# Convolution kernels made between expert tiles, idle matmuls, and experts joined with their combine in one block

## What is computed

```python
x = x + tanh(g_xattn[i]) * attention_i(layernorm(x), ctx)
x = x + tanh(g_ffn[i]) * ffn_i(layernorm(x))
...
eh = gelu(ln(ctx @ hist_W + hist_b))
aw = softmax(gelu(eh @ ctx_W1 + ctx_b1) @ ctx_W2 + ctx_b2)
cc = sum(eh * aw)
kp = gelu(ln(cc @ kg_W1 + kg_b1)) @ kg_W2 + kg_b2
kernels = softmax(kp.reshape(B, H, 9))
```

## Time and profile before

| what | value |
|---|---|
| median of 3 runs | 862.2 us |
| the profiled execution | 863.15 us |
| its span, first to last instruction | 861.4 us |
| mean granted TensorE clock, share of 2.4 GHz | 0.851 |
| busy: PE, PEld, DVE, ACT, POOL | 73%, 55%, 49%, 34%, 27% |

### The profile page before, as it was taken

How to read it: one execution, slowest core, us unless ns; L and a number is a source line. 1 busy time by engine, 2 the same in 40 slices (tenths; PEclk the granted TensorE clock), 3 DMA queues, 4 the chain that set the end, 5 groups by cost and what they waited for, 6 DMA issues and landing times. The chain is left out here.

```text
span 861.4 us, 14476 instructions
## 1 busy us (share of the span) xinstructions
PE 625.5 (73%) x4568; PEld 474.8 (55%) x4569; DVE 419.9 (49%) x1096; ACT 289.5 (34%) x826; POOL 230.0 (27%) x275
## 2 busy tenths in 40 slices
PE   4888679775199999927963799833977999528771
PEld 2556566455189999913652366511544666414441
DVE  3674456783633333265956233247644453352333
ACT  1285223772044444303420233320631444202220
POOL 2033010132145553110000466303400111115651
PEclk9999899898589999967965899955886999757996
DMA  7970000000110010018500111010000000001122
GB/s 230 356 290 1 1 0 1 2 1 7 38 30 26 25 24 18 13 56 320 172 0 25 34 41 41 27 49 2 1 0 2 2 2 2 5 27 40 43 40 85
DMA packets 28984, 44.77 MB, mean 52 GB/s; under 512 B 5458, under 2 KB 18402, under 8 KB 28674
## 3 DMA queue, kind: packets, MB, share of 16 engines
q1 hardware_dynamic: 24514, 35.02, 12.2%
q0 software_dynamic: 4416, 9.05, 4.1%
HBM read 37.44 MB, written 6.62 MB: 51 GB/s over the span
## 5 line engine op out<-in xcount | busy, mean ns | idle before, releaser
L1105 PE MATMUL experts_ps<-experts_act,experts_own 128*128 128x128 f32 x736 | 86.0, 275 | 0.2 <-ACT experts_act L1160 0.2
L1285 PE MATMUL gated_ps_in<-experts_w_in,gated_slots_t 128*128 x138 | 75.5, 659 | 13.4 <-issue 5.7
L1105 PEld LDWEIGHTS experts_ps<-experts_act,experts_own 128*128 128x128 f32 x736 | 84.0, 192 | 0.3 <-issue 0.3
L1160 ACT ACTIVATE experts_act<-experts_ps,experts_b 128x128 f32<-128x128 f32 x184 | 52.6, 369 | 72.1 <-PE experts_ps L1105 57.4
L1038 POOL DMA_INDIRECT gated_slots<-ffn_tokens,keep_ffn_token x46 | 44.6, 969 | 72.8 <-issue 46.6
L1196 DVE COPY experts_own<-experts_w 128x2048 f32 x23 | 28.2, 1226 | 64.5 <-PE experts_ps L1105 64.5
L642 POOL TENSOR_TENSOR core_e<-core_e,core_inverse 128x1024 f32<-128x1024 f32 x16 | 30.4, 1902 | 103.6 <-DVE core_inverse L787 103.6
L1029 POOL DMA_INDIRECT ffn_results<-gated_results,keep_ffn_row x46 | 45.4, 986 | 37.6 <-DVE gated_results L1381 28.7
L1038 POOL DMA_INDIRECT experts_slots<-ffn_tokens,keep_ffn_token x23 | 36.8, 1599 | 63.1 <-PE experts_ps L1086 41.2
L1371 DVE COPY gated_slots_t<-gated_ps_x 128x128 f32<-128x128 f32 x46 | 13.4, 292 | 82.5 <-PE gated_ps_x L1277 72.3
L1304 PEld LDWEIGHTS gated_ps_y<-experts_w_out,gated_gated_t 128*128 128x128 f32 x276 | 35.9, 197 | 24.4 <-issue 24.4
(11 more groups left out here) (390 smaller groups left out, 1372.6 us busy)
## 6 DMA issues: line engine op xcount, KB each, us to landing
experts_w<-in_L_ffn_W SPq DMA_DIRECT2D x1, 8192.0 KB, 40.2
experts_w_in<-in_gated_in SPq DMA_DIRECT2D x1, 4096.0 KB, 12.3
combine_mine<-ffn_results SPq DMA_DIRECT2D x12, 256.0 KB, 3.5
experts_w<-in_L_ffn_W SPq DMA_DIRECT2D x1, 2048.0 KB, 11.6
experts_w_out<-in_gated_out SPq DMA_DIRECT2D x1, 2048.0 KB, 17.2
ffn_tokens<-route_xn SPq DMA_DIRECT2D x3, 512.0 KB, 3.2
experts_w_in<-in_L_ffn_gate_w SPq DMA_DIRECT2D x1, 1024.0 KB, 7.6
experts_w_in<-in_L_ffn_up_w SPq DMA_DIRECT2D x1, 1024.0 KB, 10.4
```

The lines of the kernel that those rows point to most:

```text
L1105: mm = pe.matmul(ps_2[u][:, c * P:(c + 1) * P], own2[:, u, k, c * P:(c + 1) * P], act1[:, u, k, :], start=(k == 0), stop=(k == chunks - 1))
L1160: act.activation(to[:, u, c, :], source[u][:, c * P:(c + 1) * P], ACT.Gelu, bias=bias[:, bass.ds(e * chunks + c, 1)]).then_inc(done, 1)
L1285: mm = pe.matmul(ps_in[:, banks * u + n], slots_t[:, u, :], w_in[:, bass.ds(e, 1), 512 * n:512 * n + 512].rearrange("d a h -> d (a h)"), s ...
```

## The change

1. `conv_kernels` becomes a class `ConvKernels` whose pieces are called between expert tiles of layer 1's `gelu_experts`. PE has ten pieces, at steps j = 1, 4, 5, 6, 9, 10, 11, 14, 15 and 18, each behind `layer3(j - 2)`; ACT has five (2, 4, 6, 12, 15), DVE thirteen, POOL three (behind the gathers 0, 8 and 18). For this, the loops of PE, ACT and DVE there are written out. It has two PSUM banks instead of eight. The weights for it (13 DMAs, `ConvWeights.load`) are issued by SP in layer 1's `route`, behind the store of the tokens, no longer in the attention of layer 2.
2. `gated_experts` and the combine behind it share one block (`Together`), in layers 2 and 3.
3. `idle_matmuls(pe, keep, bank, times)`: matmuls of 128 x 128 fp32 whose result nobody reads: 16, 10 and 30 in each of three `route`s, 14 at the start of each of three expert stages, 16 in `lora_ffn`, 40 at the end of `latent_operands`.
4. The normalisation in `wide_attention` (attentions 0 and 1) takes `scalar_tensor_tensor` with rstd spread over the row as a second tensor.

```diff
+def idle_matmuls(pe, keep, bank, times):
+    for _ in range(times):
+        pe.matmul(bank[:, 0:P], keep.identity[:], keep.iota[:], start=True, stop=True)
...
-                    dve.tensor_scalar(xn[:, t % ring, :], keep.x[:, t, :], moments[:, t, 0:1], rstd[:, t:t + 1],
-                                      ALU.subtract, ALU.mult).then_inc(sem["xn_ready"], 1)
+                    dve.scalar_tensor_tensor(out=xn[:, t % ring, :], in0=keep.x[:, t, :], scalar=moments[:, t, 0:1],
+                                             in1=rstd[:, t:t + 1].to_broadcast([P, D]), op0=ALU.subtract, op1=ALU.mult)\
+                        .then_inc(sem["xn_ready"], 1)
...
                     .then_inc(sem["tokens_stored"], 16)
+                if load_ahead:
+                    load_ahead(sp)
                 sp.wait_ge(sem["tokens_stored"], 16)
...
             def _(pe):
+                idle_matmuls(pe, keep, ps[:, 2], 16)
                 norm.tensor(pe)
...
                 mm.then_inc(sem["logits_made"], 1)
+                idle_matmuls(pe, keep, ps[:, 2], 10)
                 pe.wait_ge(sem["chosen_ready"], 1)
...
                     .then_inc(sem["counted"], 1)
+                idle_matmuls(pe, keep, ps[:, 2], 30)
                 pe.wait_ge(sem["order_ready"], 1)
...
+                idle_matmuls(pe, keep, ps_y, 14)
                 turn_slots(0, 0, 0, True)
                 layer1(0, 0, True)
                 turn_slots(1, 1, 0)
                 turn_slots(2, 2, 0)
...
-                with pe.Fori(1, (TILES - 3) // 4) as i:
-                    for v in range(2):
-                        steady(i, v)
+                for j in range(1, TILES - 2):
+                    layer1(j, j % 2, j == 1)
+                    layer2(j - 1, (j - 1) % 2, j <= 2)
+                    turn_slots(j + 2, (j + 2) % AHEAD, (j + 2) // AHEAD)
+                    if j >= 2:
+                        layer3(j - 2, j % 2, j == 2)
+                    kernels.tensor(pe, j)
...
+                for j in range(1, TILES - 1):
+                    gelu1(j + 1, (j + 1) % 2)
+                    gelu2(j, j % 2, j == 1)
+                    kernels.scalar(act, j)
...
+                for j in range(1, TILES - 2):
+                    own_weights(j + 1, (j + 1) % 2)
+                    keep_slots(j + 2, j % 2)
+                    if j >= 2:
+                        keep_result(j - 2, (j - 2) % AHEAD, (j - 2) // AHEAD)
+                    kernels.vector(dve, j)
...
+class ConvKernels:
...
+    def tensor(self, pe, j):
...
+        if j == 9:
+            pe.wait_ge(sem["aw_ready"], 1)
+            for u in range(2):
+                mm = pe.matmul(ps[:, 0, u:u + 1], self.aw[:, 2 * u:2 * u + 2, :].rearrange("p b k -> p (b k)"), self.one[:],
+                               start=True, stop=True)
+            mm.then_inc(sem["cols_made"], 1)
...
+    def scalar(self, act, j):
...
+        if j == 6:
+            act.wait_ge(sem["aw_centred"], 1)
+            act.activation(self.aw[:], self.aw[:], ACT.Exp).then_inc(sem["aw_exp"], 1)
...
                 mm.then_inc(sem["v_made"], 1)
+                idle_matmuls(pe, keep, ps[:, 2], 40)
...
-                    gated_experts(nc, keep, "gated2", keep.routes[1], w_in2, w_out2, loaded2, 32)
-                with Together(nc), Scope(nc, "combine2") as c:
-                    conv_kernels(nc, keep, "kernels3", conv_weights, taps, Combine(keep, c, keep.routes[1]), rows3)
+                with Together(nc) as block, Scope(nc, "combine2") as c:
+                    combine = Combine(keep, c, keep.routes[1])
                     gated_experts(nc, keep, "gated2", keep.routes[1], w_in2, w_out2, loaded2, 32)
+                    block.sync(combine.load)
+                    combine.add(block, rows3)
...
-            gated_experts(nc, keep, "gated3", keep.routes[2], w_in3, w_out3, loaded3, 48)
-        with Together(nc) as block, Scope(nc, "combine3") as c:
-            combine = Combine(keep, c, keep.routes[2], out)
-            combine.add(block)
+            with Together(nc) as block, Scope(nc, "combine3") as c:
+                combine = Combine(keep, c, keep.routes[2], out)
+                gated_experts(nc, keep, "gated3", keep.routes[2], w_in3, w_out3, loaded3, 48)
+                combine.add(block)
```

468 lines of the change are left out of this document (221 added, 247 removed).

## The result

| what | before | after |
|---|---|---|
| median | 862.1 us (4 runs, 858.91 to 863.43) | 840.45 us (4 runs, 839.9 to 842.73) |
| profiled execution's span | 861.4 us | 840.9 us |
| mean granted TensorE clock | 0.851 | 0.919 |
| busy: PE, PEld, DVE, ACT, POOL | 73, 55, 49, 34, 27% | 81, 63, 50, 35, 27% |

The ratio is 0.9754, with a 95% interval of 0.9731 to 0.9777: 21 us less. The forecast was 827, 35 us less; the time lies 1.6 us inside the slow end of its range (842).

A forecast was written before the change was run, and what follows sets the result against it. No single bound: PE in layer 1's experts, chains of small steps at seams and routes, and PE's low clock behind waits. Terms -21.0 + 6.0 - 2.0 - 16.5 - 1.5 = -35.0 from 863.15 give 828.1, 827 against the median; range 814 to 842.

The forecast's parts named there:

- part 4: Layer 3's combine in the experts' block: its load goes out at 848.7 instead of 850.8, -2.0 us (0 to -3).
- Part 1: Between layer 2's experts and layer 3's attention: the convolution kernels' block goes, the combine stays, gain 21.0 us (19 to 22).
- keeps its 2.85 us: After layer 2's combine, the way into layer 3's attention, a branch on the mask, takes 2.85 us as before.
- Part 2: Convolution kernels' work moved into layer 1's experts, where PE is the limit: +6.0 us, bounds 5 and 13.2.
- So nothing waits: Layer 1's experts: DVE and ACT have 3 us free per tile, so the pieces cause no waits.
- Part 3: Layer 1's experts: writing the loops out changes nothing, 0 us; results come 5.47 us apart either way.
- Part 5: Idle matmuls in routes, `lora_ffn`, layer 2's attention and expert starts raise PE's clock: -16.5 us (0 to -20).
- The clock need not fall: Layer 1's route: 16, 10 and 30 idle matmuls take 3.9, 2.4 and 7.2 us and fit their gaps.
- rival (b): Idle matmuls do no harm but give little, since DVE or a DMA sets each start: 840 us, chance 0.14.
- Part 6: Wide attentions: normalisation with two tensors takes 0.35 us where three took up to 1.97, -1.5 us (0 to -5).
- Rival (d): Loops: waits in layer 3's experts may hang on code position, and go (818) or reach another loop (838); chance 0.14.

The follow-up runs named there:

- the load ahead: Changed kernel with layer 2's combine loads issued in the experts' block and its adds in a block of their own: 840.4 us, ratio 0.975.
- the jump taken out: Changed kernel, joined block kept, without the attention for any mask that is jumped over when the mask is causal: 837.6 us, ratio 0.979.

## Why the prediction came out as it did

The direction and the main cause were right; the size was not: 21 us instead of 35. The time is inside the range, but near its end: the two largest terms and two of the others all erred to the slow side, and only part 4 gave more than forecast. By its own steps:

- **Part 1 (-21.0): -18.0 measured**, 39.25 to 21.24 us from the last result to the attention. Load, landing and combine came as worked out, the load even 0.7 us sooner. The step that failed is "keeps its 2.85 us": it is 6.43, and 6.41 to 6.43 in all eight profiles with the joined block and the jump. The forecast took the end of the combine's block as it was. But the joined block ends with the long DRAIN on POOL, 3.84 us behind POOL's last work, where the combine's own block has 0.06. The join did not remove this time, it moved it from ahead of the load to ahead of the attention. That the indirect DMAs call for it is the likeliest reading, since only the blocks with them have it; no run leaves them out, and what POOL does in that time no record shows.
- **Part 2 (+6.0): +7.9 measured** from first to last result, and 0.9 ahead of it: +8.8, inside its bounds. Records of PE in the pieces:

```profile
243.00:372.00 129.00, 7.32 (x41) 4.70 (x41) 4.02 (x11) 0.47 (x1) 1.00 0.08 21
```

  They are 7.32 us (the piece of j = 1 included) where half of 13.22 is 6.6, and the latency at the end of a piece, which the forecast gave to other matmuls to cover, isn't given back: the step with the piece of j = 9, four small records of 0.60 us in all, is 0.73 us longer than 5.47. "So nothing waits" failed once, at j = 2: the normalisation on DVE waits for POOL, and the next weights come behind it.

```profile
257.15 0.73 DVE L1647 TENSOR_SCALAR experts_eh<-experts_eh,experts_eh_moments,experts_eh_rstd 128x256 f32<-128x256 f32 x2 [2.56 <-POOL experts_eh_rstd L1535]
...
260.04 1.13 PE L1109 MATMUL experts_ps<-experts_slots_t,experts_own 128*128 128x128 f32 x8 [0.75 <-issue]
```

  That cost 1.0 us over two steps. The place where a wait was most likely, the Exp with its two table loads at j = 6, held as worked out (ACT's timeline):

```profile
284.82 1.28 ACT L1615 ACT_TABLE_LOAD   x1
286.11 0.42 ACT L1615 ACTIVATE experts_aw<-experts_aw 1x256 f32<-1x256 f32 x1
286.55 1.28 ACT L1167 ACT_TABLE_LOAD   x1
287.84 2.43 ACT L1167 ACTIVATE experts_act<-experts_ps,experts_b 128x128 f32<-128x128 f32 x8
```

  1.28 + 0.42 + 1.28 = 3.0 us, and the two results behind it come 5.47 us apart as in the loop. The Trainium skill gives 2.66 us per switch, of which 1.38 are a drain ("ScalarE: Activation LUTs", What ACT_TABLE_LOAD costs). This trace has the 1.28 us of the load and no drain: each instruction in these lines starts 0.01 to 0.02 us behind the one before.
- **Part 3 (0): 0**, shown by the run without pieces. The Trainium skill says that a taken branch stalls an engine when its target lies outside the fetched window ("Runtime: NRT & Kernel Launch", Instruction fetch mechanics). The forecast counted this loop's branch as such a one; with the loop and without it the stage takes 115.13 us, so there was no stall to win back. Whether the target lies in the window no run here shows.
- **Part 4 (-2.0): -2.8** (5.44 to 2.65 from last result to load). Here nothing stands behind the block but the program's end, so nothing is given back inside the span: POOL's DRAIN (827.42 to 832.46) runs beside the load and the adds, which last until 838.06.
- **Part 5 (-16.5): 7 to 8 measured**, in both directions. This is the term that missed most. The forecast priced each place by itself: so many records at the low clock, so many at the full one. Two steps of it failed. "The clock need not fall" in route 1: it stayed full through the 32 idle records and the turns, and was at 0.50 from 216.7 to 223.5. The logits took 2.72 us instead of 3.52, but the 10 idle ones behind them 4.61 instead of the 2.4 of the forecast, and the counting, whose input was ready at 221.54, began at 222.77. So the route went from 20.85 to 20.90 in that profile. (The turns take 2.09 us at the full clock and 2.23 at the low one, since they follow DVE's tiles, 2.15 us.) And the gain of a place as gain of the whole: in `lora_ffn` the first 16 records took 1.95 us as forecast, but the 8 of L2747 behind them 3.46 instead of 1.99, and attention 1 gave back the rest. Where the forecast saw the idle matmuls fit (5.8 us in route 3) they took 6.65, and the turn began 2.3 us behind the first xn tile instead of 0.45 as before; with 9 instead of 16 the whole was not faster. The rival (b), "they give little", gave 840 and a chance of 0.14; it was the nearest case, but that its number was met is luck: it took a quarter of the gain, half was there, and parts 1, 2 and 6 made up the rest.
- **Part 6 (-1.5): 0.** The long normalisation isn't a matter of the instruction's form, so the change did not touch it. The row that was to tell it, the adds of the earlier trace rows at 0.35 us, are of the same form but never ran beside POOL's multiplication, so they could not show that the form helps.

The sum of what was measured, -18.0 + 8.8 - 2.8 - 7.5, is -19.5, against 21 in the medians. In the pair of profiles 2.3 us come from attention 3, which the change doesn't touch and which takes 149.4 to 152.7 us in all profiles but one.

Rival (d), loops that stall: layer 3's waits moved neither with the change nor with the position of the code. At the two times at which the kernel before took 862 us every profile shows them, and 60.7 to 62.8 us from first to last result of experts 3; at the three at which it took 854 to 856 none does, and the stage takes 53.4 to 53.9. In the changed kernel's first profile (waits in layer 3's experts: us, times, longest):

```profile
DVE gated_slots_t L1365 <- remote: 9.2, 3, 3.6
...
ACT gated_gated_t L1345 <- remote: 6.2, 3, 2.8
```

and the busy time of the same stage, from first to last result, there and in the same kernel run again:

```profile
766.10:827.20 61.10, 45.21 (x189) 25.40 (x189) 18.77 (x63) 16.02 (x42) 36.82 (x38) 0.94 0.16 40
```
```profile
768.30:821.40 53.10, 42.88 (x189) 23.54 (x188) 18.40 (x61) 15.78 (x42) 36.39 (x38) 1.00 0.18 46
```

The same 189 matmuls, 8 us apart, about as much as the medians differ (862 and 856 before, 840 and 835 changed). So they are no term of the change. What the waits are is open, and so is what they go with: runs with them (the normalisation moved, the load ahead) and without them (the changed kernel again, the jump taken out) were recorded under the same chip number.

## What to carry to other kernels

Joining two blocks saves a wait only if the end of the block gets off the path; look for what that end costs (here 3.8 us of POOL's DRAIN in a block with indirect DMAs) and let a transfer land beside it: the load issued inside and the work behind it outside beat both joined and apart by 3.9 and 2.7 us at the seam. Idle matmuls are worth their gain in the next few microseconds, less what they delay and less what the clock takes back one stage later: half of the sum over the places here, so measure them as a set. A move of latency-bound work into a stage that one engine bounds costs its full records on that engine, small ones included, and is worth it all the same when it removes more of a chain than that (18.0 us won for 8.8).

## What the runs showed of the hardware

- POOL's DRAIN at the end of a block ends 3.82 to 3.84 us behind POOL's last work in the blocks with 46 indirect DMAs, and 0.05 to 0.08 us behind it in all others in which POOL works (all 14 profiles). With the last indirect DMA 12 us back it is as long.
- Normalisations on DVE that begin within 0.02 us behind the start of POOL's 128 x 1024 multiplication (1.90 us) end 0.08 us (`tensor_scalar`) or 0.15 us (`scalar_tensor_tensor`) after it, in 1.97 and 2.04 us instead of 0.35. Those that begin 0.16 us ahead of it take 0.26, and put 1.3 us ahead of it, 0.34 to 0.35. Removing the long ones gave only 0.5 us a step.
- The granted clock can differ between two executions of the same instructions: 0.57 and 1.00 in the 4 us from the first scores of attention 1 on, and 1.2 us in the seam. So a seam moves by up to 3 us from profile to profile (attention 2: 58.6 to 61.5), and an edit of 2 us can be seen in its seam while the median doesn't tell it.
- Layer 3's experts took 53.4 to 53.9 us at some times and 60.7 to 62.8 at others, with the same program in the stage, and the profiles of one time were alike. The runs don't show what it goes with.
